# Moving the first half's routing of a cross-attention and expert kernel to other engines and to a later stage

## The reference

```python
# cross attention: queries from the normalised x; keys and values from context and x together
ln = layer_norm(norm(x), g_l, b_l); xn = layer_norm(ctx, g_x, b_x)
q = ln @ Wq; k, v = split(concat([xn, ln], axis=1) @ Wkv)      # 16 heads of 64, 512 keys
out = (softmax(mask(q @ k.T / 8)) @ v) @ Wout
x = x + layer_norm(out, g_o, b_o)                              # first normalisation
# experts
xf = norm(x).reshape(1024, 128)                                # second normalisation
aff = xf @ centroids.T                                         # 64 experts
idx = top_k(aff + expert_biases, 8)
w = sigmoid(aff[idx]); w = w / (sum(w) + 1e-8); cw = scatter(w, idx)
shared = silu(xf @ Ws_up) @ Ws_down
routed = sum_e cw[:, e] * (silu(xf @ W_up[e]) @ W_down[e])     # all 64 experts are computed
x = x + shared + routed
```

## Time and profile before

| | us |
|---|---|
| median of 3 runs (427.53 to 430.43) | 429.78 |
| the profiled execution | 426.99 |
| its span, first to last instruction | 424.8 |
| TensorE busy | 356.2 (84%) |
| VectorE busy | 336.9 (79%) |
| ScalarE busy | 274.9 (65%) |
| GpSimd busy | 220.9 (52%) |
| mean granted TensorE clock | 0.962 of full |

### The profile page before, as it was taken

The page is one execution under the profiler, slowest core; times in us unless marked ns, Lnnn a source line. Parts: engine busy times, 40 slices in busy tenths (PEclk is TensorE's granted clock), DMA queues, the critical chain, the costliest instruction groups (busy, mean ns, idle before and its releaser), DMA issues.

```text
span 424.8 us, 7546 instructions
## 1 busy us (share of the span) xinstructions
PE 356.2 (84%) x2369; PEld 238.7 (56%) x2369; DVE 336.9 (79%) x818; ACT 274.9 (65%) x611; POOL 220.9 (52%) x253
## 2 busy tenths in 40 slices
PE   0279687999999999995868998588766979999995
PEld 0157354666666666663545765365443656677773
DVE  2989677878778778789798768854999999788874
ACT  3468777787787778775555958355333777767672
POOL 4233405888878887859645786479992100000000
PEclk9999999999999999999698999699969999999999
DMA  8200212989698978997656486461000000000000
GB/s 243 66 0 1 51 25 49 171 135 183 128 159 137 185 156 127 167 184 152 111 92 136 75 124 99 77 113 38 2 0 0 0 2 1 2 25 0 2 0 25
DMA packets 121127, 34.44 MB, mean 81 GB/s; under 512 B 110976, under 2 KB 120704, under 8 KB 121088
## 3 DMA queue, kind: packets, MB, share of 16 engines
q1 hardware_dynamic: 120656, 32.39, 42.9%
q10 hardware_dynamic: 432, 1.57, 1.1%
HBM read 8.26 MB, written 0.52 MB: 21 GB/s over the span
## 4 chain that ended last, share of the span: by engine, by line
PE 47%; DVE 26%; issue 8%; POOL 6%; DMA 6%; ACT 6%; SPq 1%; DVEq 0%; ACTq 0%; POOLq 0%
PE ps L717 8%; PE ps L761 7%; PE ps L652 5%; PE ps L654 4%; PE ps L653 4%; DMA pT<-p 4%; PE ps L786 3%; POOL p L375 3%; PE ps L893 3%; DVE v L1138 3%; DVE h_lo L1327 3%; DVE sc L1095 3%; PE ps L895 3%; PE ps L873 3%; PE ps L894 3%
## 5 line engine op out<-in xcount | busy, mean ns | idle before, releaser
L375 POOL TENSOR_TENSOR p<-prob,p 128x512 f16<-128x512 f32 x96 | 111.5, 1162 | 7.7
L1095 DVE CUSTOM_DVE_ANT_0 sc<-ps,mask_add 128x512 f32<-128x512 f32 x128 | 83.3, 688 | 33.2 <-PE ps L717 29.9
L373 POOL CAST p<-prob 128x512 f16<-128x512 f32 x96 | 58.6, 610 | 71.7 <-ACT prob L489 58.3
L489 ACT ACTIVATE prob<-sc,p_bias 128x512 f32<-128x512 f32 x128 | 91.5, 716 | 3.0 <-POOL p L375 1.0
L497 ACT ACTIVATE p_bias<-neg_max,ln_range 128x2 f32<-128x2 f32 x64 | 18.6, 290 | 60.6 <-DVE neg_max L1095 60.6
L621 ACT ACTIVATE h_hi<-h 128x512 fp32r<-128x512 f32 (+1 forms) x66 | 41.3, 625 | 24.8 <-DVE h L1320 24.6
L608 ACT ACTIVATE h<-ps 128x512 f32<-128x512 f32 (+1 forms) x66 | 39.3, 595 | 26.8 <-PE ps L654 26.5
L1320 DVE TENSOR_TENSOR h<-h,ps 128x512 f32<-128x512 f32 x64 | 43.9, 685 | 14.0 <-PE ps L873 13.7
L761 PE MATMUL ps<-pT,v 128*64 128x256 f16 x768 | 50.7, 284 | 0.0
L1327 DVE TENSOR_TENSOR h_lo<-h,h_hi 128x512 fp32r<-128x512 f32 (+1 forms) x66 | 48.5, 734 | 0.9 <-ACT h_hi L621 0.8
L717 PE MATMUL ps<-k_hi,q_hi 64*128 64x512 f32 x128 | 33.0, 511 | 18.8 <-DVE neg_max L1095 17.8
(11 more groups left out here) (180 smaller groups left out, 761.0 us busy)
## 6 DMA issues: line engine op xcount, KB each, us to landing
wup_s<-in_L_ffn_W_up SPq DMA_DIRECT2D x8, 256.0 KB, 3.8
wdn_s<-in_L_ffn_W_down SPq DMA_DIRECT2D x8, 256.0 KB, 3.8
pT<-p SPq DMA_TRANSPOSE x96, 3.2
wkv_s<-in_L_xattn_Wkv ACTq DMA_DIRECT2D x2, 512.0 KB, 5.9
x_in<-in_x SPq DMA_DIRECT2D x2, 256.0 KB, 7.2
tok<-in_ctx SPq DMA_DIRECT2D x4, 128.0 KB, 8.0
wq_s<-in_L_xattn_Wq ACTq DMA_DIRECT2D x1, 512.0 KB, 8.3
wo_s<-in_L_xattn_Wout SPq DMA_DIRECT2D x1, 512.0 KB, 5.3
```

Source lines behind the costliest of these rows:

```text
L373: pool.tensor_copy(p16[:, t, 0, :], prob[:, t, :]).then_inc(s_phi, 1)
L375: pool.tensor_tensor(p16[:, t, 1, :], prob[:, t, :], p16[:, t, 0, :], ALU.subtract).then_inc(s_plo, 1)
L489: act.activation(prob[:, t, :], sc[:, t, :], ACT.Exp, bias=p_bias[:, t:t + 1], scale=-1.0, accum_out=p_sum[:, i % 2, t:t + 1]).then_inc(s_ ...
L1095: return dve.tensor_tensor_reduce(sc[:, t, :], ps[:, score_bank(i, t), :], mask_add[:, step(i)[2], :], -SCALE, -LEAST, ALU.add, ALU.min, n ...
```

## The change

The first half's routing is taken off VectorE where it can be and most of it out of the steps. In the steps stay the output transposes and moments (step 20) and the first normalisation: ScalarE takes the inverse root as exp(-ln(v)/2) (`root2`) and applies scale and shift (`normalise_turned`), GpSimd does one Newton correction (`refine`) and the residual. The moments of the sum come at the end of step 31. The second normalisation, input transposes, affinities, selection and gates come after it. In the second half's routing, too, GpSimd does the Newton iterations (three in `refine`) and the residual, between parts of the expert weights, and ScalarE the normalisations; the entries at which its pieces stand are later. The gates take Sigmoid on ScalarE instead of Exp, an addition and a reciprocal. `x_res` and `b_o` are loaded at the end of the opening's loads and added there. `h` and the buffers keep their places; `biased` moves next to `x_res`.

```diff
 sync, opening
+            sp.dma_start(x_res[:, :, :], x.rearrange("b (q p) d -> p (b q) d", p=P)).then_inc(s_xin, 16)
+            sp.dma_start(bo_row[:, :], row(b_o).broadcast_to([P, P])).then_inc(s_xin, 16)
 load_late
-                sp.dma_start(x_res[:, :, :], x.rearrange("b (q p) d -> p (b q) d", p=P)).then_inc(s_late, 16)
-                sp.dma_start(bo_row[:, :], row(b_o).broadcast_to([P, P])).then_inc(s_late, 16)
 gpsimd
+            pool.wait_ge(s_xin, 32)
+            pool.tensor_tensor(x_res[:, :, :], x_res[:, :, :], bo_row[:, :].unsqueeze(1).broadcast_to([P, NT, P]), ALU.add)\
+                .then_inc(s_xres, 1)
...
+            def refine(n, times):
+                at = 4 * n
+                r, v, t, m = rs[:, at:at + 4], tmp[:, 0, at:at + 4], tmp[:, 1, at:at + 4], shift[:, at:at + 4]
+                for _ in range(times):
+                    link(pool.tensor_tensor(t, r, r, ALU.mult))
+                    linked()
+                    link(pool.tensor_tensor(t, t, v, ALU.mult))
+                    linked()
+                    link(pool.tensor_scalar(t, t, -0.5, 1.5, ALU.mult, ALU.add))
+                    linked()
+                    link(pool.tensor_tensor(r, r, t, ALU.mult))
+                    linked()
+                link(pool.tensor_tensor(m, r, mv[:, at:at + 4, 0], ALU.mult))
+                linked()
+                pool.tensor_scalar(m, m, -1.0, None, ALU.mult).then_inc(s_rs, 1)
+
+            def residual(half):
+                pool.wait_ge(s_late, LATE)
+                pool.wait_ge(s_xn, half + 1)
+                link(pool.tensor_tensor(outN[:, :, :], outN[:, :, :], go_row[:, :].unsqueeze(1).broadcast_to([P, 4, P]),
+                                        ALU.mult))
+                linked()
+                pool.wait_ge(s_xres, 1)
+                pool.tensor_tensor(x1[:, 4 * half:4 * half + 4, :], outN[:, :, :], x_res[:, 4 * half:4 * half + 4, :],
+                                   ALU.add).then_inc(s_added, 1)
             for i in range(STEPS):
                 for t in range(DMA_TILES):
                     split(i, t)
-                if i == FIRST + 4:
-                    ... x_res + bo_row
-                if i == FIRST + 8:
-                    split_shared()
-                if i == FIRST + 11:
-                    xf_low(0)
+                if i == FIRST + 5:
+                    pool.wait_ge(s_std2, 1)
+                    refine(0, 1)
+                if i == FIRST + 6:
+                    residual(0)
...
+            split_shared()
+            pool.wait_ge(s_std2, 2)
+            refine(1, 1)
             for part in range(FT // 4):
...
+                if part == 0:
+                    xf_low(0)
+                if part == 1:
+                    pool.wait_ge(s_var2, 3)
+                    refine(2, 3)
+                if part == 2:
+                    residual(1)
+                if part == 3:
+                    pool.wait_ge(s_var2, 4)
+                    refine(3, 3)
             xf_low(1)
 scalar
+            def root2(n):
+                cut = slice(4 * n, 4 * n + 4)
+                act.wait_ge(s_var2, n + 1)
+                act.activation(rs[:, cut], tmp[:, 0, cut], ACT.Ln).then_inc(s_act, 1)
+                act.wait_ge(s_act, n + 1)
+                act.activation(rs[:, cut], rs[:, cut], ACT.Exp, scale=-0.5).then_inc(s_std2, 1)
+            def normalise_turned(half):
+                act.wait_ge(s_rs, 2 * half + 1)
...                 four ACT.Identity of 128x128 with bias shift and scale rs, into outN
+            def expert_input(half):
+                act.wait_ge(s_rs, 2 * half + 2)
...                 four ACT.Identity of 128x128 from x1 into xh
             for i in range(1, STEPS):
+                if i == FIRST + 5:
+                    root2(0)
                 if i + 1 < STEPS:
                     k_high(i + 1)
...
                 exp(i, 3)
+                if i == FIRST + 5:
+                    normalise_turned(0)
+                if i in (FIRST + 7, FIRST + 12):
+                    fill_selector((i - FIRST) // 12)
+            root2(1)
             last_high(STEPS - 1)
+            expert_input(0)
+            evac_xf(0)
+            xf_high(0)
+            sigmoid(0)
...  expert loop on ScalarE: fill_selector at n = 2 and 8, normalise_turned(1) at 4, expert_input(1) at 14,
...  evac_xf(1) at 17 (was 12), xf_high(1) at 18 (was 13), sigmoid(1) at 22 (exp_affinity was at 17)
 tensor, i = 32 and 33 are the two steps that finish the attention
+                if i == STEPS:
+                    pe.wait_ge(s_qlo, STEPS // 2)
                     turn_input(0)
+                if i == STEPS + 1:
                     affinities(0)
-                if i == STEPS:
-                    up(0)
-                    up(1)
+            project(STEPS - 1)
+            up(0)
+            up(1)
             up(2)
-            project(STEPS - 1)
+            up(3)
+            turn_gates(0)
+            turn_out(1)
             spread(1)
-            up(3)
+            up(4)
             spread(2)
-            up(4)
-            turn_out(1)
...  loop: turn_input(1) at n = 16 (was 11), affinities(1) at 20 (was 14), turn_gates(1) at 27 (was 22)
 vector
                 if i == FIRST + 4:
                     moments(turned(0), 0)
-                    start_root(0)
-                if i == FIRST + 5:
-                    newton(0, 3)
-                if i == FIRST + 6:
-                    centre(0)
-                    residual(0)
-                if i == FIRST + 7:
+                    variance(0)
+                if i == STEPS - 1:
+                    dve.wait_ge(s_added, 1)
                     moments(x1_of(0), 4)
-                    start_root(4)
-                if i == FIRST + 8: newton(4, 3), expert_input(0)
-                if i == FIRST + 12 to FIRST + 15: bias_affinity(0), find(0), gates(0), gate_parts(0), take_gates(0)
+                    variance(4)
             invert(STEPS - 1)
             last_low(STEPS - 1)
             normalise_out(STEPS - 2)
             normalise_out(STEPS - 1)
+            bias_affinity(0)
+            find(0)
+            gates(0)
+            gate_parts(0)
+            take_gates(0)
...  loop: moments(turned(1), 8) and start_root(8) at n = 0; moments(x1_of(1), 12) and start_root(12) at n = 9;
...  newton, centre, residual and expert_input are gone; bias_affinity(1) at 21 (was 16), find(1) at 22 (17),
...  gates(1) at 24 (18), gate_parts(1) at 25 (19), take_gates(1) at 28 (23)
```

More of the change, by code:

```diff
@@ L536, in evac_out @@
                 act.wait_ge(s_wout, STEPS // 2 * (half + 1))
-                if half:
-                    act.wait_ge(s_cw, 1)
                 act.activation(outT[:, :], ps[:, OUT_BANK, :], ACT.Copy).then_inc(s_outT, 1)
@@ L557, in xf_high, with sigmoid @@
                 act.activation(xf_hi[:, half * 512:(half + 1) * 512], xfT[:, :], ACT.Copy).then_inc(s_xfhi, 1)
-            def exp_affinity(half):
+            def sigmoid(half):
                 act.wait_ge(s_biased, half + 1)
@@ L563, in exp_affinity @@
                 act.activation(gate[:, :, :].rearrange("p j e -> p (j e)"), ps[:, (Q_BANK, NEXT_BANK)[half], 0:4 * E],
-                               ACT.Exp, scale=-1.0).then_inc(s_expd, 1)
+                               ACT.Sigmoid).then_inc(s_sigmoid, 1)
+            def root2(n):
[6 more added lines that the diff above has]
+                act.wait_ge(s_rs, 2 * half + 1)
+                if half:
+                    act.wait_ge(s_cw, 1)
+                for j in range(4):
+                    at = 8 * half + j
+                    source = ps[:, NEXT_BANK, j * P:(j + 1) * P] if half else outN[:, j, :]
+                    ins = act.activation(outN[:, j, :], source, ACT.Identity, bias=shift[:, at:at + 1],
+                                         scale=rs[:, at:at + 1])
+                ins.then_inc(s_xn, 1)
+            def expert_input(half):
+                act.wait_ge(s_rs, 2 * half + 2)
+                for j in range(4):
+                    at = 8 * half + 4 + j
+                    ins = act.activation(xh[:, j, :], x1[:, 4 * half + j, :], ACT.Identity, bias=shift[:, at:at + 1],
+                                         scale=rs[:, at:at + 1])
+                ins.then_inc(s_xh, 1)
             for i in range(1, STEPS):
@@ L1168, in start_root, with variance @@
                 chained()
-                chain(dve.tensor_scalar(r.bitcast(I32), t.bitcast(I32), -1, MAGIC, ALU.mult, ALU.add))
-            def newton(at, times):
-                r, v, t = rs[:, at:at + 4], tmp[:, 0, at:at + 4], tmp[:, 1, at:at + 4]
-                for _ in range(times):
-                    chained()
-                    chain(dve.scalar_tensor_tensor(out=t, in0=r, scalar=-0.5, in1=r, op0=ALU.mult, op1=ALU.mult))
-                    chained()
-                    chain(dve.tensor_tensor(t, t, v, ALU.mult))
-                    chained()
```

(9 more changed lines are left out.)

154 lines of the change are left out of this document (51 added, 103 removed).

## The result

The changed kernel took 417.4 us (median of 4 runs, 416.1 to 418.6) and the kernel before 428.7 beside it: a ratio of 0.973, with a 95% interval of 0.967 to 0.979. The forecast was 410, in a range of 398 to 425. The profiled execution took 418.59 us (span 416.8).

| stage | before, us | after, us | difference | forecast |
|---|---|---|---|---|
| start to the reciprocal of step 2 | 81.02 | 82.58 | +1.6 | 0 |
| steps 2 to 16, no routing | 87.68 | 87.64 | 0 | 0 |
| steps 16 to 30, routing | 113.26 | 94.39 | −18.9 | −18.6 |
| step 30 to the end of entry 0 | 16.55 | 25.23 | +8.7 | +9 |
| entries 0 to 33 | 72.69 | 73.40 | +0.7 | −10.0 |

A forecast was written before the change was run, and what follows sets the result against it. TensorE bounds steps without routing; in-order VectorE's routing work stalls it in later steps and the early expert loop. Terms −18.6 + 9 − 10.0 = −19.6 us take 426.99 to 407.4; with 2.8 for the median, about 410 us, range 398 to 425.

The forecast's parts named there:

- The steps: Attention steps with routing: 25.6 us of routing cost removed, 7.0 kept (bounds 3 and 12), a gain of 18.6 us.
- The opening: Start of the kernel: the added 512 KB load and GpSimd addition cost nothing; without cover the addition costs 2.36 us.
- The drain's start: Last exponent to third weight spread: the first half's remaining routing now stands there, +9 us (bounds 6 and 13).
- The rest of the expert loop: Expert entries after the drain's start: 17.7 us removed against 7.7 us of new losses, −10.0 us.
- the 7.7 us of new losses: Expert loop: late weight parts, VectorE's moments and root starts, and selection and gates cost 7.7 us (bounds 3 and 14).
- the 17.7 us taken as removed: Expert loop: 14.7 us lost beside VectorE's second-half normalisations and about 3 us around the gates go away.
- 2.7, 1.2 and 2 us: Expert loop: TensorE's losses because GpSimd splits weight parts 3, 4 and 5 late.
- GpSimd becomes the bound: Rival: forty small dependent GpSimd operations on the path; at 1.0 us each 439 us, slower than before; chance 0.08.
- the forecast's own sign: In the changed profile, the forecast is wrong if a small GpSimd operation takes over 0.5 us.
- The steps don't come back to pace: Rival: transposes or GpSimd bind once VectorE is free, the steps keep 13 us: 416 to 424 us; chance 0.06.
- More than forecast: Rival: every lower bound holds in steps, drain's start and loop: 398 us or below; chance 0.08.
- Half of it: Rival: same mechanism at 0.5 us a small GpSimd operation: 419 us, up to 428 with drain's start at bound; chance 0.12.

The follow-up runs named there:

- e3: Changed kernel with ScalarE's first-half normalisation and GpSimd's residual one step later: 411.7 us, ratio 0.958 to the kernel before.
- e1: Changed kernel with GpSimd's four places in the expert loop two weight parts later, and what hangs on them two entries later: 409.5 us, ratio 0.953.
- e2: Changed kernel without two of the three Newton passes of each of the second half's two inverse roots: 411.9 us, ratio 0.957.
- f1: e8 with TensorE turning the first half's expert input ahead of the last attention again, as in the changed kernel: 399.2 us, ratio 0.934.
- f5: f1 with the second half's two inverse roots made by VectorE instead of GpSimd: 414.5 us, ratio 0.972.
- f4: Changed kernel with VectorE, not GpSimd, making the Newton passes and shifts of the second half's two inverse roots: 418.6 us, ratio 0.976.
- e8: Changed kernel with later first-half normalisation and loop places, third weight part behind the gates, shared split in step 24, input turning behind last attention: 400.1 us, ratio 0.936.
- f3: Changed kernel with VectorE making the steps' remaining inverse root at the end of step 20, instead of ScalarE and GpSimd: 418.6 us, ratio 0.977.

## Why the prediction was right, and where it was not

**The steps** (7.0 us kept, 6.7 measured). The mechanism was as forecast: ScalarE waits for GpSimd's correction, once, and the pace returns. A small operation cost 0.27 us (0.28 forecast), the loads of the table were two, and by e3 neither mattered much beside the wait. Inside the sum one thing was small: TensorE stood 4.64 us, not 2.2 to 3.2. GpSimd came to the correction at 203.08, not 200.4; 1.5 of that is the opening, which shifts all that follows, and 1.2 us are its own, since its wait for transposes was 3.19 us, hardly shorter than the 3.51 before, although two loads had moved. ScalarE's key copy then came 6.4 us late by the same count, and only 1.8 of that was slack, not 3.1. So steps 21 and 22 cost 6.5 us, not 5.5. (Of these 5.5 us the sum has 3.5 and 2.0, but its own list gives 3.7 to 5.2 for stall and clock together and nothing for the products of step 22, which were indeed hidden: that step took 6.92 us, an undisturbed one 7.21.) The last step, 2.0 us shorter than the undisturbed one of its kind, made up for it. That sum and measurement agree to 0.3 us is partly luck, since step 21 alone took 10.3 to 12.9 us in other executions (e3).

The forecast estimated 4 us more by the price of the Trainium skill ("ScalarE: Activation LUTs", What ACT_TABLE_LOAD costs), 2.66 us a switch. The trace doesn't agree: the rows show 1.28 for a load and an activation right behind each (192.03, 193.55). By e3 the two loads cost some 0.4 us of step 20, near the 0.5 that the sum has for them.

**The opening** (0, measured +1.6). The 1.6 us can't be put down to the change: the same opening came up to 1.7 us earlier in other executions, as early as that of the kernel before. That the 2.36 us of the addition find cover there is shown by the 8.30 us for which GpSimd stands behind it.

**The drain's start** (+9, measured +8.7) went by its steps: correction 1.62 us (1.7), then the transposes ahead of the last attention, at a granted clock of 0.59 from 274.9 to 279.8 us, and about 21 us to the third spread.

**The rest of the expert loop** (−10.0, measured +0.7) is the step that failed, in the 7.7 us of new losses. Against the 17.7 us taken as removed they were 18.4, outside their own bounds of 3 and 14; that the time still lies in the range is owed to the range's width, not to this step. I named the right waits: GpSimd stands for the variance, about 10 us, and TensorE for its weight parts. But 2.7, 1.2 and 2 us became 7.7, 0 and 8.4. Three things were missed.
- For part 3 the variance came 4.9 us after the third spread (3.8 forecast), and the correction took 5.4 us, not 3.9, since four of its 14 operations took about 0.6 us beside VectorE.
- For part 5 I wrote "about 2" and didn't work it out. VectorE makes that variance in its turn 9 of the loop (n = 9), and TensorE wants part 5 in its turn 12: about three entries, 5.2 us. But the variance was ready only 4.2 us after TensorE began turn 9, and 5.0 us of correction and 1.9 of splitting came behind it.
- I counted no clock behind these stops, though I had for the step: 10.8 us of the 16 are idle time, the rest is matmuls at the lower clock.

e1 shows that the places were the cause (73.40 to 59.02 us for these entries), e2 that the chains' length is some 6 us of it. The 59.02 us are 13.7 less than in the kernel before, so most of the 17.7 us which I took as removed were there to be had.

The Trainium skill ("SBUF — State Buffer", Who interferes with whom) said that VectorE and GpSimd take turns, and I estimated 3 us by it. The trace agrees: seven of the 28 small operations in the loop took 0.56 to 0.61 us instead of 0.20, 2.7 us together. The forecast read the rule as speaking against the move. By f1 and f5 it speaks for it: VectorE's small operations wait for GpSimd's long ones, on the engine that TensorE waits for. That is 15 us between f1 and f5, of which two undisturbed chains would make up some 4 us, by the 2.11 us that TensorE waited for f4's first.

**The rivals.** *GpSimd becomes the bound* fell: its small operations cost 0.27 us in the steps and 0.37 in the loop, against the 0.78 from which it would decide. By the forecast's own sign, a small operation of over 0.5 us, those seven count against it, but they are 2.7 us in all. *The steps don't come back to pace* fell: steps 23 to 29 together took 0.8 us more than undisturbed ones. *More than forecast* didn't come either, though e8 and f1 show that a time near 399 was there to be had. *Half of it* named a time near the measured one, but by dearer operations, which isn't what happened. Its far end of 428 doesn't follow either: with the bound of the drain's start, 4 us more, it is 423.

## What to carry to other kernels

When work moves to an engine that takes its list in order, write down for each wait what is queued behind it and when that is wanted, entry by entry, as one does for the engine that was relieved; places two parts later were worth 14 us of the loop here. Price small dependent operations by what the other engine does beside them, not by their undisturbed rows. And before taking an idle wait away, look at what ran undisturbed because of it: here it was the gates.

## What the hardware showed that I had not expected

Small operations suffer more from sharing on VectorE than on GpSimd here: VectorE's operation on four columns goes from 0.16 us to 0.5 and 1.1 (f3, f4, f5), GpSimd's from 0.20 to 0.6. One such operation of 1.31 us stood in the earlier trace rows; what I had not expected is that a whole chain pays. In f4 and f5 it moves in step with GpSimd's casts (0.6 us) and products (1.27 us), so 11 operations that take 2.1 us beside an idle GpSimd take 5.7 to 7.0. And the clock granted in the opening differs between executions of kernels that are alike there, 0.66 against 0.83 from 50 to 60 us, which is 1.7 us of a single time.
